# A windowed attention step on VectorE: one row buffer of 66 columns in place of two of 65, and a new order of the step

## The reference

```python
q_local = feature @ wq_w + wq_b
def step(buf, q_i):                                   # buf: the last 64 rows v
    ki = concatenate([buf, zeros((B, 1, D))], axis=1) # 65 rows
    scores = einsum('bwd,d->bw', q_i[:, None, :] * ki, w2_w) + w2_b[0]
    alpha = softmax(scores, axis=1)
    v_i = einsum('bwd,bw->bd', ki, alpha)             # the new row
    return concatenate([buf[:, 1:, :], v_i[:, None, :]], axis=1), v_i
_, vs = scan(step, feature[:, :64, :], transpose(q_local[:, 64:, :], (1, 0, 2)))
```

## Time and profile before

| what | value |
|---|---|
| median of 3 runs | 2812.13 us (2804.04 to 2821.11) |
| the profiled execution, its own time | 2813.75 us |
| its span, first to last instruction | 2812.0 us |
| VectorE busy | 2212.6 us, 79% of the span |
| ScalarE busy | 1285.9 us, 46% |
| TensorE busy (matmuls) | 1182.1 us, 42% |

### The profile page before, as it was taken

The page is one execution under the profiler, slowest core; times in us unless marked ns, Lnnn a source line. Parts: engine busy times, 40 slices in busy tenths (PEclk is TensorE's granted clock), DMA queues, the critical chain, the costliest instruction groups (busy, mean ns, idle before and its releaser), DMA issues. The chain is left out here.

```text
span 2812.0 us, 40923 instructions
## 1 busy us (share of the span) xinstructions
PE 1182.1 (42%) x7272; PEld 524.0 (19%) x7272; DVE 2212.6 (79%) x16135; ACT 1285.9 (46%) x3230; POOL 288.5 (10%) x425
## 2 busy tenths in 40 slices
PE   3010000101010010101004887878877777788796
PEld 1000000000000000000001111224321333223365
DVE  5999999999999999999975799776767667765133
ACT  1333333333333333333360456657854675577742
POOL 0000000000000000000010020032123210311211
PEclk8555555555555555555555799889997898899898
DMA  5000000000000000000034021103120221000100
GB/s 138 1 1 1 1 1 1 1 1 1 1 1 1 1 1 1 1 1 1 1 75 99 1 57 31 20 22 90 33 45 21 68 52 32 23 22 28 42 1 23
DMA packets 80203, 66.31 MB, mean 24 GB/s; under 512 B 8702, under 2 KB 64808, under 8 KB 79944
## 3 DMA queue, kind: packets, MB, share of 16 engines
q1 hardware_dynamic: 76872, 57.40, 8.4%
q0 software_dynamic: 3072, 6.30, 0.7%
HBM read 34.77 MB, written 28.57 MB: 23 GB/s over the span
## 5 line engine op out<-in xcount | busy, mean ns | idle before, releaser
L1332 DVE TENSOR_REDUCE nm_half<-pair 128x2 f32<-128x1024 f32 x512 | 611.8, 1220 | 197.9 <-PE pair L1580 186.4
L209 ACT ACTIVATE ex<-row,nmax 128x65 f32<-128x65 f32 x960 | 336.1, 350 | 891.8 <-DVE row L274 799.3
L1220 ACT ACTIVATE pt<-pair 128x1024 f32<-128x1024 f32 x512 | 513.4, 1025 | 383.8 <-PE pair L1590 370.6
L269 DVE SCALAR_TENSOR_TENSOR junk<-ex,tab 128x65 f32<-128x65 f32 x2850 | 618.1, 220 | 1.8 <-issue 1.1
L389 PE MATMUL p_s<-tab,bdg 128*128 128x32 f32 x120 | 31.8, 406 | 809.5 <-DVE tab L274 809.5
L1556 PE MATMUL p_o<-pt,va 128*9 128x512 f32 x2048 | 299.3, 659 | 7.0 <-ACT pt L1220 7.0
L274 DVE SCALAR_TENSOR_TENSOR tab<-rz,raw 128x1 f32<-128x1 f32 (+1 forms) x1890 | 293.7, 155 | 8.5 <-issue 2.4
L286 DVE STREAM_SHUFFLE row<-tab 128x130 f32<-128x130 f32 x930 | 280.1, 301 | 10.9 <-issue 3.1
L1580 PE MATMUL pair<-ks,qs 48*128 48x512 bf16 x1024 | 210.3, 422 | 108.7 <-ACT pt L1220 55.2
L269 DVE DVE_READ_ACCUMULATOR junk<-ex,tab 128x1 f32 x2850 | 235.4, 83 | 0.7
L1590 PE MATMUL pair<-qs,ks 50*128 50x512 bf16 x1024 | 210.5, 415 | 54.8 <-ACT pt L1220 24.8
(11 more groups left out here) (253 smaller groups left out, 2008.1 us busy)
## 6 DMA issues: line engine op xcount, KB each, us to landing
parts_dram<-parts SPq DMA_DIRECT2D x48, 256.0 KB, 3.6
qs<-parts_dram SPq DMA_DIRECT2D x32, 192.0 KB, 4.8
ks<-parts_dram SPq DMA_DIRECT2D x32, 192.0 KB, 5.2
hid<-xs_dram SPq DMA_DIRECT2D x33, 128.0 KB, 2.1
ys_dram<-hid SPq DMA_DIRECT2D x33, 128.0 KB, 1.8
h_dram<-f SPq DMA_DIRECT2D x20, 128.0 KB, 2.6
x<-in_x SPq DMA_DIRECT2D x4, 512.0 KB, 8.8
w_W<-in_W SPq DMA_DIRECT2D x1, 2048.0 KB
```

Source lines behind the costliest of these rows:

```text
L209: nc.scalar.activation(ex[:, r % 2, :], row[:, r % 2, 1, :], ACT.Exp, bias=nmax[:, r % 2:r % 2 + 1], accum_out=z[:, r % 2:r % 2 + 1]).then ...
L269: nc.vector.scalar_tensor_tensor(junk[:, g, :], ex[:, k, :], CAP, tab[:, g, r:r + ROW], ALU.min, ALU.mult, accum_out=raw[:, g:g + 1]).then ...
L1220: nc.scalar.activation(pt[:, kt % 2, :, tokens(t)], pair[fill.pair][:, :, :], ACT.Exp, scale=SCALE).then_inc(s_exp, 1)
L1332: nc.vector.reduce_max(nm_half[:, t, hp % 2, :, q], pair[fill.pair][:, :, :], AX.X, negate=True)\
```

## The change

The row of a step is kept once, 66 columns wide: columns 0 to 64 are what the unshifted copy held, columns 1 to 65 what the shifted one held. The shuffle copies 66 columns in place of 130. The maximum reads 65 columns. Since the new score is now written into the same buffer that the maximum reads, it waits for the maximum (`s_max`) too. The step's order becomes: maximum, reciprocal, weighted 0, raw new score, coefficients of the step before, score for the table, new score, weighted 1, shuffle, weighted 2.

```diff
-        row = sb("row", [P, 2, 2, ROW])
+        row = sb("row", [P, 2, ROW + 1])
...
-                    nc.scalar.activation(ex[:, r % 2, :], row[:, r % 2, 1, :], ACT.Exp, bias=nmax[:, r % 2:r % 2 + 1],
+                    nc.scalar.activation(ex[:, r % 2, :], row[:, r % 2, 1:], ACT.Exp, bias=nmax[:, r % 2:r % 2 + 1],
...
             def shifted(q, r):
 
-                src = tab[:, 0, r:r + ROW]
-                pair = bass.AP(src.tensor, src.offset, [src.ap[0], [1, 2], [1, ROW]])
-                nc.vector.stream_shuffle(row[:, q % 2, :, :], pair, [q] * L).then_inc(s_row, 1)
+                nc.vector.stream_shuffle(row[:, q % 2, :], tab[:, 0, r:r + ROW + 1], [q] * L).then_inc(s_row, 1)
 
             def largest(c, r):
                 dve.wait_ge(s_row, L * c + r + 1)
-                nc.vector.reduce_max(nmax[:, r % 2:r % 2 + 1], row[:, r % 2, 0, 1:], AX.X, negate=True)\
+                nc.vector.reduce_max(nmax[:, r % 2:r % 2 + 1], row[:, r % 2, 1:], AX.X, negate=True)\
                     .then_inc(s_max, 1)
...
                     dve.wait_ge(s_exp, n + 1)
+                    if not last:
+                        largest(c, r + 1)
+                    nc.vector.reciprocal(rz[:, k:k + 1], z[:, k:k + 1]).then_inc(s_rz, 1)
+                    if not last:
+                        weighted(0, k, r, s_raw_score)
+                    if not last:
+                        dve.wait_ge(s_row, n + 2)
+                        nc.vector.scalar_tensor_tensor(junk[:, 3, :], ex[:, k, :], CAP, row[:, 1 - k, 0:ROW], ALU.min,
+                                                       ALU.mult, accum_out=raw[:, 3:4]).then_inc(s_raw_new, 1)
                     if r:
                         coefficients(c, r - 1)
-                    nc.vector.reciprocal(rz[:, k:k + 1], z[:, k:k + 1]).then_inc(s_rz, 1)
                     if not last:
-                        dve.wait_ge(s_row, n + 2)
-                        nc.vector.scalar_tensor_tensor(junk[:, 3, :], ex[:, k, :], CAP, row[:, 1 - k, 0, :], ALU.min,
-                                                       ALU.mult, accum_out=raw[:, 3:4]).then_inc(s_raw_new, 1)
-                    if not last:
-                        largest(c, r + 1)
-                    if not last:
-                        weighted(0, k, r, s_raw_score)
+                        dve.wait_ge(s_raw_score, m)
+                        divided(tab[:, 0:1, r + WIN:r + ROW], 0, 1, k, s_score)
                     if not last:
                         dve.wait_ge(s_raw_new, m)
                         dve.sem_inc(s_pace, 1)
                         dve.wait_ge(s_rz, n + 1)
-                        divided(row[:, 1 - k, 1, WIN - 1:WIN].unsqueeze(2), 3, 4, k, s_new)
+                        dve.sem_inc(s_pace, 1)
+                        dve.wait_ge(s_max, n + 2)
+                        divided(row[:, 1 - k, WIN:ROW].unsqueeze(2), 3, 4, k, s_new)
                     if r:
                         dve.wait_ge(s_coef, n)
                     weighted(1, k, r, s_raw)
-                    if not last:
-                        dve.wait_ge(s_raw_score, m)
-                        divided(tab[:, 0:1, r + WIN:r + ROW], 0, 1, k, s_score)
-                    weighted(2, k, r, s_raw)
                     if r < L - 2:
                         dve.wait_ge(s_score, m)
                         dve.sem_inc(s_pace, 1)
                         shifted(r + 2, r + 1)
+                    weighted(2, k, r, s_raw)
```

More of the change, by code:

```diff
@@ L298, in _ @@
                 dve.sem_inc(s_pace, 1)
-                nc.vector.stream_shuffle(row[:, 0, 1, :], tab[:, 0, 0:ROW], [0] * L).then_inc(s_row, 1)
+                nc.vector.stream_shuffle(row[:, 0, 1:], tab[:, 0, 0:ROW], [0] * L).then_inc(s_row, 1)
                 shifted(1, 0)
                 dve.wait_ge(s_row, L * c + 1)
-                nc.vector.reduce_max(nmax[:, 0:1], row[:, 0, 1, :], AX.X, negate=True).then_inc(s_max, 1)
+                nc.vector.reduce_max(nmax[:, 0:1], row[:, 0, 1:], AX.X, negate=True).then_inc(s_max, 1)
                 dve.wait_ge(s_bdc, c + 1)
```

## The result

The changed kernel takes 2985.11 us (median of 4 runs, 2976.73 to 2985.91) where the kernel before takes 2816.24 (median of its 4 runs beside it): a ratio of 1.060, 95% interval 1.056 to 1.064. That is 169 us more; 179 were forecast, and 2991 us for the whole.

A forecast was written before the change was run, and what follows sets the result against it. VectorE's order was taken to bind at 1.31 us a step; after the change the circle, with two exposed waits, at 1.495. Waits 172 plus edges 7 gave 179 us on 2813.75, 2993, less 1.6: 2991 us, range 2880 to 3045.

The forecast's parts named there:

- VectorE's order: VectorE's own instructions in one step, start to start: 0.55 plus 0.76, together 1.31 us, said to bind the kernel before.
- the circle: New score to exp on ScalarE and back to VectorE's next new score: 1.21 us before, at least 1.28 or 1.29 after.
- The two separate waits: Ahead of the new score: first wait 0.155 us, second 0.11, making the step 1.495 us, +172 us over 930 steps.
- The shuffle: Behind the new score: 130 to 66 columns saves 0.06 us, but covered by exp, so it cannot shorten the step.
- B: Rival: ahead of the new score the second wait passes together with the first; step 1.385 us, 2889 us; chance 0.14.
- C: Rival: waits cost nothing, only operations count; step 1.28 to 1.29 us, 2791 to 2800 us; chance 0.09.
- D: Rival: next step's row comes late for the maximum; +28 to +79 us on top, about 3044 us; chance 0.15.
- the edges: First and last steps of each chunk: 5 to 8 us, +2 us, less 2 us for the first wide shuffle; sum +7.
- stalls stay: Stalls were said to stay as they are, along with GpSimd's work, chunk heads and the second layer; no time added.
- The idle time ahead of the new score: Sign: VectorE idle about 0.26 us between raw sum's accumulator read and new score, charged to its own write.

The follow-up runs named there:

- the third wait: Changed kernel with a third separate wait ahead of the new score, for the long-passed row: 3085.46 us, ratio 1.097 to the kernel before.
- the order alone: Changed order with the old two copies and 130-column shuffle, one separate wait and no wait for the maximum, against the kernel before: 2873.45 us, ratio 1.023.
- the first three runs: Changed kernel with one separate wait ahead of the new score (2873.76 us), with none (2786.46 us), and with three (3085.46 us).
- the last one: Changed layout, four operations and no separate wait ahead of the new score, coefficients at step's end, against the kernel before: 2674.52 us, ratio 0.951.

## Why the prediction was right

The step that carried it held: which of two bounds sets the step. VectorE's order set it before, with about 0.10 to spare on the circle; the change shortens what is not on the circle and lengthens what is.

- **The circle.** Forecast 0.835 from the maximum to the new score and 0.66 from there to the next maximum; the step shown has 703.37 - 702.54 = 0.83, and the whole is 1.50 against 1.495. Without the two waits it has 1.29, as the operations alone were forecast to take.
- **The two separate waits.** Forecast 0.155 for the first and 0.11 for the second; measured 0.15 with one and 0.26 with two. The one term that no row of before showed, the second wait with nothing to wait for, was the largest single cause: 111 us of the 169 go when it alone goes. It had been taken between bounds as the passing without the waiting, and that is what the third wait confirmed (0.11 once more, where it was known to be passed). The reason given for choosing 0.155 over 0.10 was not the right one: 0.155 was put down to VectorE's own write. In the trace of the kernel before, the wait's record starts 0.04 after the write in both places, behind VectorE (L298, ahead of L300) and behind ScalarE (L310, ahead of L313); what differs is the time from that record to the next instruction, 0.116 and 0.071. The first also raises a semaphore, the second does not.
- **The shuffle.** Forecast worth nothing in the new order, since exp covers it: the order alone and the same order with one wait and the small shuffle differ by 0.3 us (2873.45 and 2873.76). In the old order the layout is worth 60 us (2809 to 2749), which also shows that the circle had at least 0.07 to spare there.
- **Rivals.** B (the second passes with the first) and C (waits are free) fall to the first three runs; D (the next row late) did not come about, since the maximum starts 0.03 behind the exp.
- **The size.** 179 forecast for the loop, 169.65 measured. The starts of the 960 exps in both traces take the 10 us apart. The median step inside a chunk grows from 1.310 to 1.496, by 0.186 where 0.185 was forecast: 173 us for 930 steps. The first step of a chunk grows by another 0.13 (4 us in all, 5 to 8 forecast), and the joints between chunks change by under 1 us together, so that the edges are worth 3 and not 7. The other 7 are in a term that was put at nothing, "stalls stay": what the steps take beyond the median falls from 30 to 23 us, for a reason that no run shows. That the whole came out within 6 us of the forecast (2985 against 2991) is in part the chance of single runs; the profiled execution, at 2976.73, lies 16 under its own forecast of 2993.
- **A sign that was put wrongly.** The idle time ahead of the new score was to be charged to VectorE's own write and to be 0.26 long. The score for the table runs in it, so only some 0.12 is idle (113.0 us / 930), and the view puts no name to most of it.

The Trainium skill's rule that a semaphore costs nothing extra (VectorE: DVE Perf Modes, The DRAIN you can't avoid) does not carry over to a wait that is an instruction of its own: here each such instruction, with the `sem_inc` that it holds, adds 0.11 us where nothing covers it. Another page of the Trainium skill (Perfetto Trace Analysis, Sequencer-only Instruction (DRAIN, etc)) says that of such an instruction the profile reports the execution alone, and that the wait before it and the update behind it are outside. The trace agrees for the added wait, whose record is 21 ns long, a fifth of what it costs:

```profile
L327 DVEq EVENT_SEMAPHORE  x930: 21/21/21, 52.1 to 1568.1; - x186
```

It does not agree for a record that waits for two semaphores: that of L287, shown in the last section, lasts up to 661 ns, nearly all of it waiting for the second.

## What to carry to other kernels

When two engines hand a small step back and forth, add up both the busier engine's order and the circle through both before moving work: what is taken off the engine pays only while the engine's order is the longer, and what stands ahead of the hand-over is in the circle in full. Count separate waits like operations, also those that are already passed, and spread them: give each of the operations ahead one wait to carry, and let the last one carry the wait that comes last. Doing without the two separate waits alone takes 199 of the 311 us between the changed kernel and the last one; the other 112 came with its order. Both together turn the same layout from 6% slower into 5% faster.

## What the runs showed of the hardware

A separate wait on VectorE of the kind used ahead of the new score, a `sem_inc` that holds a wait, takes 0.11 us once its semaphore is there, five times its record of 21 ns (0.15, 0.26 and 0.37 us from a write to the dependent instruction with one, two and three of them). The trace's records of the changed kernel's step above show them one behind the other: the raw sum is written at 703.108, the first wait starts at 703.147, the second at 703.258, the new score at 703.366. The medians of all 930 steps are 0.039, 0.111 and 0.108. So the first shows 0.04 more because its semaphore is seen 0.04 after the write.

A separate wait without a `sem_inc` was cheaper: 0.071 from the start of its record to the next instruction, in nearly all of the 30 at the heads of the chunks (L310 of the kernel before, 0.10 from the exp's end). And two of that kind are not two instructions. In a chunk's first step of the changed kernel three waits stand ahead of the maximum; it carries one, and the other two share one record, which in the first chunk starts at 50.649, 0.04 after the row is written, and lasts until 51.310, 0.04 after the exp's end:

```profile
L287 DVEq EVENT_SEMAPHORE  x930: 21/21/661, 50.6 to 1567.2; - x186
```

So what was said ahead of the prediction, that each further wait becomes an instruction of its own, does not hold for these two, which have no `sem_inc` between them. Every wait that the experiments added or left out held a `sem_inc`; none left out the `sem_inc` alone. Whether the increment is what makes 0.11 of 0.07, and what the changed kernel would take with its waits but without the two `sem_inc`, was not tested.

A mask load ahead of a shuffle can start together with it, where its wait has passed (713.96 and 713.96 in the last experiment); one that followed a wait stood 0.02 ahead of the shuffle at 731.37 in the kernel before:

```profile
731.35 0.01 DVE L300 LOAD_MASK_SELECT row<-tab  x1 [0.15 <-DVE tab L296]
```
